# A two-layer graph network: slots, keys and table parts take other places in the prologue, and counts reach the columns by DMA

## The reference, cut to what matters

```python
h = jnp.maximum(_layernorm(x, axis=-1), 0.0)
# layer 0: an MLP per edge, summed per receiver, an MLP per node
e = jnp.concatenate([edge_attr_64, h[src], h[dst]], axis=-1)
e = relu(relu(e @ We1 + be1) @ We2 + be2) @ We3 + be3
agg = segment_sum(e, dst)
x = x + mlp3(concatenate([h, agg]))
h = jnp.maximum(_layernorm(x, axis=-1), 0.0)
# layer 1: 8 softmax heads per edge; each edge's value h[dst] * edge_weight is summed into src
q = softmax((h @ u)[src] - (h @ u)[dst] + c)
y = sum_m segment_sum(q[:, m:m+1] * h[dst] * edge_weight, src) @ var_w[m]
x = x + y + var_b
```

## Time and profile before

| | us |
|---|---|
| median of 3 runs | 2374.38 |
| the profiled execution, whole | 2375.3 |
| its span, first to last instruction | 2373.6 |
| DVE busy | 1422.4 (60%) |
| PE busy | 1700.9 (72%) |
| POOL busy | 1625.3 (68%) |
| ACT busy | 555.3 (23%) |

### The profile page before, as it was taken

The page is one execution under the profiler, slowest core; times in us unless marked ns, Lnnn a source line. Parts: engine busy times, 40 slices in busy tenths (PEclk is TensorE's granted clock), DMA queues, the critical chain, the costliest instruction groups (busy, mean ns, idle before and its releaser), DMA issues.

```text
span 2373.6 us, 53585 instructions
## 1 busy us (share of the span) xinstructions
PE 1700.9 (72%) x10041; PEld 1192.6 (50%) x10041; DVE 1422.4 (60%) x6161; ACT 555.3 (23%) x1979; POOL 1625.3 (68%) x1700
## 2 busy tenths in 40 slices
PE   5698888899899989989845555555655555565554
PEld 5455555555555555556434444444444444444444
DVE  5334434444434444343358888788888888888885
ACT  2233333333333333332111111111111111111110
POOL 2777777777777777774456766667676766767673
PEclk7799999988989898898555555555555555555555
DMA  2544444444444444442133333333333333333332
GB/s 68 120 99 100 96 97 99 98 94 96 100 93 102 98 98 95 96 103 52 38 109 90 94 90 93 89 91 93 91 92 92 92 90 90 94 90 92 92 91 57
DMA packets 353203, 216.99 MB, mean 91 GB/s; under 512 B 284700, under 2 KB 325751, under 8 KB 352926
## 3 DMA queue, kind: packets, MB, share of 16 engines
q0 software_dynamic: 66800, 113.26, 21.0%
q1 hardware_dynamic: 284692, 102.18, 17.9%
q10 hardware_dynamic: 1684, 1.24, 0.2%
HBM read 209.80 MB, written 6.69 MB: 91 GB/s over the span
## 4 chain that ended last, share of the span: by engine, by line
DVE 28%; issue 25%; POOL 17%; PE 16%; DVEq 7%; DMA 6%; ACT 1%; POOLq 0%; SPq 0%; ACTq 0%
POOL X L581 16%; DMA X<-table_src,slot_s 4%; DVE EQW L1134 4%; DVE EQW L1140 3%; DVEq L1199 3%; PE bank L1363 3%; PE bank L1346 2%; DVE EX L1180 2%; DVE OT L976 2%; DVE r L1172 2%; DVE r L1176 2%; PE bank L1372 2%; DVE r L1167 2%; PE bank L1354 2%; DVE OE L1185 2%
## 5 line engine op out<-in xcount | busy, mean ns | idle before, releaser
L589 POOL DMA_INDIRECT G<-table_node_and_list,slot_s x825 | 796.1, 965 | 378.5 <-issue 210.6
L581 POOL DMA_INDIRECT X<-table_src,slot_s x825 | 789.6, 957 | 295.3 <-issue 234.4
L1482 PE MATMUL bank<-Q,G 125*64 125x128 f32 x1650 | 414.9, 424 | 183.6 <-DVE Q L1193 183.6
L1482 PEld LDWEIGHTS bank<-Q,G 125*64 125x64 f32 x1650 | 313.7, 221 | 196.4 <-issue 125.9
L1346 PE MATMUL bank<-filler 128*128 128x384 bf16 x1100 | 377.1, 343 | 1.6 <-issue 1.6
L990 DVE TENSOR_TENSOR sT<-sT,bank 65x16 f32 x275 | 46.2, 168 | 551.7 <-PE bank L1382 513.6
L1493 PE MATMUL bank<-R,w_z 65*64 65x64 f32 x1104 | 133.9, 316 | 278.2 <-DVE sT L1201 278.2
L976 DVE TENSOR_SCALAR OT<-KBT,base_p 48x375 bf16<-48x375 int32 x550 | 231.7, 422 | 65.6 <-issue 35.2
L1493 PEld LDWEIGHTS bank<-R,w_z 65*64 65x64 f32 x1104 | 122.9, 224 | 282.5 <-issue 281.2
L1363 PE MATMUL bank<-XT,w_ex 128*64 128x375 f32 x550 | 254.3, 547 | 7.5 <-issue 7.5
L1372 PEld LDWEIGHTS bank<-w,H 65*125 65x125 f32 x1650 | 232.3, 200 | 0.0
(11 more groups left out here) (168 smaller groups left out, 2072.5 us busy)
## 6 DMA issues: line engine op xcount, KB each, us to landing
KBT<-in_dst SPq DMA_DIRECT2D x550, 70.3 KB, 2.1
X<-in_edge_attr SPq DMA_DIRECT2D x275, 93.8 KB
HK<-keys SPq DMA_DIRECT2D x275, 93.8 KB
X<-table_src,slot_s POOLq DMA_INDIRECT x825
G<-table_node_and_list,slot_s POOLq DMA_INDIRECT x825
BW<-table_dst_parts SPq DMA_DIRECT2D x275, 6.0 KB
UW<-table_logit_src_parts SPq DMA_DIRECT2D x275, 0.8 KB, 1.7
table_node_and_list<-sm SPq DMA_DIRECT2D x1, 1562.5 KB
```

What stands on the lines that cost most here:

```text
L581: pool.indirect_dma_start(X[:, j, q, D:2 * D], None, tA, bass.IndirectOffsetOnAxis(ap=slot_s[:, j, q:q + 1], axis=0)).then_inc(gat_a[0][j] ...
L589: pool.indirect_dma_start(G[:, j, q, :], None, tH, bass.IndirectOffsetOnAxis(ap=slot_s[:, j, q:q + 1], axis=0)).then_inc(g_gather[j], 16)
L1482: last = pe.matmul(bank[2 + j % 2][0:D, 0:WM], G[0:P, j, q, 0:D], Q[:, j % 2, q].rearrange("p m n -> p (m n)"), start=(q == 0), stop=(q == ...
```

## The change

Six things are edited, all outside of the loops.

1. ACT copies the first four groups' slots as soon as `src` has been turned, ahead of the table copies, in both branches (the other branch waits for a higher count).
2. Tables A and B come from one pass over the blocks: 25 matmuls 128 wide instead of 50 that are 64 wide. Table A is written when the pass is over. The transpose behind the window flag stands after 20 of the 25 blocks.
3. DVE splits B right behind the key computation, under a flag load of its own, ahead of `w_u`, `w_ex`, the turned weights and the two edge-key arrays.
4. ACT makes and writes the integer keys (tK) first; SP waits for them alone (`next_out`), the keys with weights (tE) come after.
5. `degrees` and its copy go; SP copies row 64 of `sT` to `deg` by one DMA (`deg_in`), for which DVE and `degree_sums` wait.
6. In `layer_norm` the product with 1/std and the maximum with 0 are one instruction, in all three places.

```diff
-        LN = ("mean", "xc", "sq", "var", "rstd", "norm", "relu")
+        LN = ("mean", "xc", "sq", "var", "rstd", "relu")
...
-        TABLES = [(s, c) for s in ("a", "b") for c in range(NOC)]
+        TABLES = [("ab", c) for c in range(NCH)]
...
-            done_act(sp, ("a", NOC - 1))
+            done_act(sp, TABLES[-1])
             sp.dma_start(tA.rearrange(nodes, p=P), tab_a).then_inc(tA_out, 16)
...
-                sp.wait_ge(keys_out, 64)
+                sp.wait_ge(next_out, 32)
                 over_groups(sp, lambda t, j: back(rows0w, t, j, 0))
...
+            sp.wait_ge(sT_ready, 1)
+            sp.dma_start(deg[:, 0, :], sT[D:DC, :].rearrange("o (p b) -> o p b", p=P)).then_inc(deg_in, 16)
             sp.wait_ge(lists_in, 16 * NB)
...
+            done_dve(act, ("turned_f", 1))
+            act.wait_ge(const_ready, CONSTS)
+            for j in range(RB):
+                act.copy(slot_s[0:P, j, :], src_i[:, j * TG:(j + 1) * TG]).then_inc(slots_ready[0], 1)
...
                 act.wait_ge(keys_ready, 1)
+                act.copy(key_int, key_raw).then_inc(keys_split, 1)
+                act.wait_ge(keys_split, 1)
+                act.dma_start(tK[0:E].rearrange("(c q p) -> q c p", q=IC, p=P), key_int).then_inc(next_out, 16)
+                act.dma_start(tK[E:].unsqueeze(0), no_key_i[:]).then_inc(next_out, 16)
                 act.copy(key_w[:, :, :, 0], key_raw)
-                act.copy(key_int, key_raw)
                 act.copy(key_w[:, :, :, 1], raw[:, 2]).then_inc(keys_split, 1)
...
-                step(dve.tensor_tensor(hs, hs, st[:, 3, b0:b1].unsqueeze(2).to_broadcast([P, b1 - b0, D]), ALU.mult))
-                done_dve(dve, ("norm", t))
-                step(dve.tensor_scalar(to, hs, 0.0, None, ALU.max))
+                step(dve.scalar_tensor_tensor(out=to, in0=hs, scalar=0.0,
+                                              in1=st[:, 3, b0:b1].unsqueeze(2).to_broadcast([P, b1 - b0, D]),
+                                              op0=ALU.max, op1=ALU.mult))
...
+            flag_ = load_flag(dve)
+            with dve.If(flag_):
+                of_b = tab_b
+                done_act(dve, TABLES[-1])
+                for k in range(PARTS):
+                    dve.tensor_copy(b_parts[:, :, k, :], of_b).then_inc(b_split, 1)
...
-            dve.wait_ge(deg_pe, 1)
-            on_deg(dve.tensor_copy(deg[:, 0, :], bank[7][0:P, 0:NB]))
+            dve.wait_ge(deg_in, 16)
...
+            for c in range(NCH):
+                if c >= 2:
+                    done_act(pe, ("ab", c - 2))
+                if c == 5:
+                    pe.wait_ge(win_dve, WIN_SPAN[0])
+                    pe.transpose(bank[4][0:1, 0:P], span[:, 0:1], ident[0:P, 0:P]).then_inc(win_pe, 1)
+                for n, b in enumerate(chunk_blocks(c)):
+                    last = pe.matmul(bank[c % 2][0:P, n * 2 * D:(n + 1) * 2 * D], hT[:, b * P:(b + 1) * P], w_ab[:],
+                                     start=True, stop=True)
...
-                for b in range(NB):
-                    last = pe.matmul(bank[7][0:P, b:b + 1], sT_of[:, b, :], ident[0:DC, D:DC],
-                                     start=True, stop=True)
-                last.then_inc(deg_pe, 1)
...
-                pe.wait_ge(deg_dve, 1)
+                pe.wait_ge(deg_in, 16)
                 pe.matmul(bank[7][0:P, NB:2 * NB], tri[:], deg[:, 0, :], start=True, stop=True)
```

More of the change, by code:

```diff
@@ L247, in build_gnn @@
         keys_ready, keys_split = sem("keys_ready"), sem("keys_split")
-        keys_out = sem("keys_out")
+        keys_out, next_out = sem("keys_out"), sem("next_out")
         hk_load = [sem(f"hk_load{j}") for j in range(RB)]
+        deg_in = sem("deg_in")
         deg_pe, deg_dve, start_ready = sem("deg_pe"), sem("deg_dve"), sem("start_ready")
@@ L594, in gathers @@
                 g = 2 * i + j
-                pool.wait_ge((slots_ready[0], slots_g)[l], g + 1)
+                pool.wait_ge((slots_ready[0], slots_g)[l], g + 1 + (RB, 0)[l])
                 pool.sem_inc(pool_go, 1)
@@ L637, in _ @@
             with pool.Else():
-                pool.wait_ge(keys_out, 64)
+                pool.wait_ge(keys_out, 32)
+                pool.wait_ge(next_out, 32)
                 pool.memset(dst_i[:, NT:], 0)
@@ L687, in _ @@
                 act.copy(hT[0:D, lo:hi], bank[c % 2][0:D, 0:hi - lo]).then_inc(act_step, 1)
[L689 to L693, removed]
+            done_dve(act, ("turned_f", 1))
[3 more added lines that the diff above has]
+            for c in range(NCH):
+                b = chunk_blocks(c)
+                done_pe(act, ("ab", c))
+                act.copy(ab[:, :, b[0]:b[-1] + 1, :], bank[c % 2][0:P, 0:len(b) * 2 * D].rearrange(
+                    "p (b h f) -> p h b f", h=2, f=D)).then_inc(act_step, 1)
             done_pe(act, "w3T")
@@ L755, in _ @@
             with act.If(flag_):
-                for j in range(RB):
-                    slots_w(0, 0, j)
                 edge_keys()
@@ L922, in _ @@
                                      op1=ALU.add).then_inc(keys_ready, 1)
+            flag_ = load_flag(dve)
[4 more added lines that the diff above has]
+                    dve.tensor_copy(b_parts[:, :, k, :], of_b).then_inc(b_split, 1)
+                    if k < PARTS - 1:
+                        dve.wait_ge(b_split, k + 1)
+                        win(dve.tensor_tensor(of_b, of_b, b_parts[:, :, k, :], ALU.subtract))
+            with dve.Else():
+                dve.sem_inc(win_dve, PARTS - 1)
             dve.wait_ge(const_ready, 2)
@@ L1012, in _ @@
             with dve.If(flag_):
[L1013 to L1019, removed]
                 over_groups(dve, body0w)
@@ L1047, in _ @@
             on_deg(dve.tensor_reduce(proof[:, 3:4], pairs[:], AX_X, ALU.add))
-            dve.wait_ge(deg_pe, 2)
+            dve.wait_ge(deg_pe, 1)
             k, from_ = 1, 0
@@ L1296, in _ @@
             done_act(pe, ("hT", NCH - 1))
[L1298 to L1304, removed]
-                last.then_inc(pe_step, 1)
[L1307 to L1313, removed]
+            for c in range(NCH):
+                if c >= 2:
[6 more added lines that the diff above has]
+                                     start=True, stop=True)
+                last.then_inc(pe_step, 1)
             done_dve(pe, ("turned", 5))
@@ L1429, in _ @@
                               ).then_inc(pe_step, 1)
-                if k == 0:
-                    degrees()
                 if k == 1:
```

8 lines of the change are left out of this document (2 added, 6 removed).

## The result

The changed kernel takes 2352.18 us in the median of 5 runs (2348.02 to 2356.60), the kernel before 2373.89 on the same chip (5 runs, 2370.86 to 2381.76): a ratio of 0.9903, 95% interval 0.9879 to 0.9927, 21.7 us less. The forecast was 20.1 us less and 2354.3 us. On a second chip the two stood at 2351.42 and 2371.81, ratio 0.9919 (0.9905 to 0.9932), 20.4 us less. The runs of one kernel spread over several us (8.6 for the changed one), so the ratio and its interval say what the change is worth, not a single run.

The account below looks back on a forecast made before the run. POOL's gather chain was taken to bound layer 0, PE the stretch between layers, DVE layer 1. Gains of 7.1 + 11.8 + 1.2 = 20.1 us off the profiled 2375.3, less 0.9, gave 2354.3 us; range 2349 to 2363.

Parts of the forecast that it names:

- Layer 0 moves as one piece with its 19th gather: In layer 0, POOL never waits for data after its 19th gather at 83.27 us, so the end shifts with that gather.
- Term A: Start of layer 0: the 19th gather goes at 76.2 us instead of 83.27, 7.1 us gained; bounds -3.1 to 9.7.
- The tables, 9.96 us: Prologue: PE's 50 table passes of 128 columns take 9.66 us plus 0.3; table A is written at 41.7 us.
- 18 gathers, 24.5 us: Layer 0's start: POOL's first 18 gathers keep their stalled length, 24.5 us, so the 19th is asked for at 76.2.
- B's write out at 53.8, SP on at 68.4: Prologue: B's parts are written from 53.8 us instead of 61.19; SP goes on 14.6 us later, at 68.4.
- What SP waits for: Before the first `HK` load: B's write takes 14.6 us, with the integer keys held back to about its end.
- the first rival: Layer 0 starts no earlier because the integer keys land last, 17.1 us from issue to `HK`; 2361 us, chance 0.16.
- `HK` to the 19th gather, 7.46: Layer 0's start: 7.46 us from SP going on to the 19th gather, as before, so it can go at 75.9.
- Term B: Between the layers: dropping `degrees` takes 11.76 us of one-column passes off PE; bounds 4.2 to 11.76.
- Term C: Normalisation between the layers: one DVE pass fewer in each half, 1.2 us gained; bounds 0.9 to 1.7.
- The clock between the layers: Rival: TensorE runs at 2.4 GHz between the layers once the one-column passes are gone; 2329 us, chance 0.03.
- Slower, PE at 1.2 GHz into layer 0: Rival: PE has no backlog and stays at the low clock into layer 0; 100 us of it give 2394, chance 0.03.

Follow-up runs that it names:

- the prologue alone: The kernel before with edits 1 to 4 only, keeping the old counts and two-step normalisation: 2366.59 us, ratio 0.9971.
- the counts alone: The kernel before with edit 5 only, the counts fetched by one DMA: 2361.23 us against 2374.80, ratio 0.9945.
- the normalisation alone: The kernel before with edit 6 only, the fused last operation of the normalisation: 2371.84 us, one time.
- late slots: The changed kernel with the copies of the first four groups' slots back behind ACT's branch: 2354.50 us, one time.
- late split: The changed kernel with B's split back behind DVE's branch and its edge keys: 2353.29 us, one time.

## Why the prediction was right

*Layer 0 moves as one piece with its 19th gather*: right. 9.2 us at the 19th gather, 9.0 at the end of layer 0.

*Term A, 7.1 us*: the mechanism held. It was 9.2 in the profiled pair and 6.9 by the ratio of the prologue alone (2374.80 x 0.0029, between 3.6 and 10.2). Whether the 2 us more are the edit's isn't shown. Three traces have the old order (the kernel before, the counts alone, the normalisation alone), with the 19th gather at 83.27, 83.60 and 80.07; three have the new one (the changed kernel twice, the prologue alone), with 74.11, 74.76 and 73.00. One pair gives 5.3, another 10.6. The steps of the term, from the first to the last:
- *The tables, 9.96 us* (50 passes, near the 9.66 that stood mostly at the lower clock). Measured 6.0 where the clock stays at 1.00 to the end of the passes (six of nine traces with wide passes), 9.1 to 10.0 where it falls at 32 to 34 us. That a pass hardly costs by its columns holds: at 0.50, 0.212 us with 64 columns (10.60 / 50), 0.234 with 128 (2.34 / 10) and 0.235 with one; in the 10.60 us the weight loads (PEld) are busy throughout. I had not asked what the clock does when the passes end sooner. In the profiled pair this term is the one that was mis-sized: table A was written at 38.64 instead of 41.7, the first gather came at 49.03 instead of 51.7. But little of it reaches the 19th gather: in the changed kernel's second trace, with 9.1 us of passes and the first gather at 50.53, it went at 74.76, still 8.5 earlier than 83.27.
- *The write of table A, 8.2 us to landing*: 8.59.
- *18 gathers, 24.5 us*: 22.9 (49.03 to the end of the 18th's slot at 71.9). The edge-key arrays fell on the first two, as said, but cost little: the second took 1.18 us. The first's 1.10 is no stall, for it took as much in the late slots, when the arrays were over. A gather that began inside a TENSOR_TENSOR took longer by what was left of that: in the kernel before 0.92 us more at 54.71, with 0.89 left, and in the late split 1.77 more, with 1.74 left. The rule on two SBUF inputs (the Trainium skill, SBUF — State Buffer, "Who interferes with whom") agrees with this: the casts of the split left gathers at 0.94, operations with two inputs took them to between 1.18 and 2.71.
- *B's write out at 53.8, SP on at 68.4*: 50.05 and 65.36, 3 to 4 us early like the tables.
- *What SP waits for*: I took B's write, with the keys held to about its end. The keys came last, the mechanism of the first rival. The price stayed, because both share the queues and end close together: with the keys 9.6 us earlier and B's write 3.2 later (late split) `HK` came no earlier. The rival's 17.1 us from tK's issue to `HK` were 11.4.
- *`HK` to the 19th gather, 7.46*: 8.75. The first `HK` was used 3.96 us after its issue instead of 2.74, which I had overlooked: tE, which edit 4 puts behind tK, is now still being written when `HK` is asked for. The row below is q10 in the changed kernel from 64 to 66 us; the kernel before has no packet on q10 from 75 to 79. In the seven traces with tE behind tK and the keys late, the first `HK` took 3.9 to 6.0 us, in the six others 2.6 to 2.9; no run moved tE alone. A second stall, 1.31 at the 22nd gather, I had ruled out; the normalisation alone has it too (1.30), in the old order. So the path over `HK` came last at the 19th gather (POOL waits 2.47 us there), and not POOL's own 18 gathers, which the forecast had last by 0.3.

```profile
q10 hardware_dynamic: 232, 0.21, 33.6%
```

*Term B, 11.76*: right (11.74 in the run with the counts alone). The DMA needs 2.8 us, near the bound of 2.1.

*Term C, 1.2*: right (1.4).

*The clock between the layers*, a chance of 0.03: half true. It doesn't go to 2.4 GHz for the stretch. It rises for some 3 us at the `w_u` passes, worth 2.5 us in the profiled run, in eight of thirteen traces and with the old passes too.

*Slower, PE at 1.2 GHz into layer 0*: no. The clock is 0.95 from the 19th gather on, 0.94 before.

The sum: in the two profiled spans 27.1 us (2373.6 to 2346.5), of which A 9.0, B 11.8, C 1.4, the clock 2.5 at the `w_u` passes and 0.6 at the first two chunks (granted 1.00 instead of 0.66 at their start) make 25.3; layer 1 was 1.5 shorter (2373.6 - 1203.92 and 2346.5 - 1178.36), and the time from layer 0's last gather to PE's first chunk 0.3. By medians 20.4 to 21.7: the profiled execution took 2348.29, 3.9 us under its median. That the forecast of 20.1 came within 2 us is partly luck: its sum has no term for the clock, which gave 3 us in this pair, and the runs spread by more than that.

## What to carry to other kernels

Moving work ahead pays only as far as what it stands behind has become shorter: the same order lost 4.5 us at the 19th gather with the old tables and gained 9 with the new. When several transfers share the queues and one wait ends with the last, ask for the sum of them and not for the one that ended last: the split's place moved the end of the wait by 1.5 us, the keys' order by 2.2, and the 19th gather by 0.1 and 1.1. A transfer that is put later falls together with what comes after it, as tE did with the first `HK`. And look at how many partitions a write has: 125 used 5 of 16 DMA engines, and cutting off 5 partitions gave 2 to 5 us more.

## What the runs showed of the hardware that was not expected

The granted clock of TensorE falls at another moment from run to run, with the same program ahead of it (at 38 and at 33 us in the changed kernel's two traces): PE goes to work at 18 us with the clock at 1.00 in every trace, and it fell at 32 to 35 us in seven traces, under the tables' passes, and at 37 to 39 in six, at their end or after it. All four traces with narrow passes are among the seven; whether the width has a part in it is open. A 128-column fp32 pass takes 0.12 us at 1.00 (4.77 / 40) and 0.234 at 0.50.
